# Causal mask of an attention block moved from TensorE to GpSimd, with one copy moved to VectorE and the first batch reordered

## The reference

```python
xn = _layernorm(x, axis=-1)
x = x + _L0_attn_ref(xn, ...) + _L0_ffn_ref(xn, ...)

# attention: 16 heads of 8 channels
qkv = x @ w_in.T + b_in
scores = einsum('bhqd,bhkd->bhqk', q * scale, k) + causal_bias    # -inf above the diagonal
out = einsum('bhqk,bhkd->bhqd', softmax(scores), v) @ w_out.T + b_out

# feed-forward: softmax router, top 2 of 8 experts of width 176, and a shared expert of width 352
g = silu(x @ w_gate) * (x @ w_up)
y = sum over experts of combine * (g @ w_down), and + shared expert
```

## Time and profile before

| | |
|---|---|
| median of 3 runs | 555.38 us (553.04, 557.18, 555.38) |
| the profiled execution, own time | 554.11 us |
| its span | 552.3 us |
| busy share PE, PEld, DVE, ACT, POOL | 93%, 58%, 78%, 60%, 42% |
| one batch (exponential of unit 0 to the next batch's) | 64.8 us: 203.98 to 268.76 |
| of it attend, from the first exponential to the end of the last | 19.2 us: 203.98 to 223.2 |
| granted PE clock, in 40 slices | 0.9 or more of full in all but the third, which has 0.7 |

### The profile page before, as it was taken

The page is one execution under the profiler, slowest core; times in us unless marked ns, Lnnn a source line. Parts: engine busy times, 40 slices in busy tenths (PEclk is TensorE's granted clock), DMA queues, the critical chain, the costliest instruction groups (busy, mean ns, idle before and its releaser), DMA issues.

```text
span 552.3 us, 16880 instructions
## 1 busy us (share of the span) xinstructions
PE 512.5 (93%) x6840; PEld 321.2 (58%) x6840; DVE 430.5 (78%) x845; ACT 330.6 (60%) x454; POOL 229.6 (42%) x201
## 2 busy tenths in 40 slices
PE   1589999999999999999999999999999999999995
PEld 1355654676557664576546664576646765467643
DVE  3989988899859968598757968599686978489713
ACT  6322489445873469544894458834696348844593
POOL 2026810587007840379005870078403790058600
PEclk9979999999999999999999999999999999999999
DMA  9887016900367005750169003770068302590000
GB/s 261 219 242 181 2 67 163 259 5 11 117 188 196 2 11 162 207 132 1 68 170 258 16 11 116 192 193 1 11 188 219 94 1 78 149 270 16 11 21 21
DMA packets 46896, 62.55 MB, mean 113 GB/s; under 512 B 6672, under 2 KB 30448, under 8 KB 46832
## 3 DMA queue, kind: packets, MB, share of 16 engines
q1 hardware_dynamic: 44124, 58.34, 38.6%
q10 hardware_dynamic: 2708, 3.24, 1.8%
HBM read 45.18 MB, written 15.34 MB: 110 GB/s over the span
## 4 chain that ended last, share of the span: by engine, by line
PE 70%; DVE 8%; ACT 7%; issue 5%; DMA 5%; POOL 4%; SPq 1%; ACTq 0%; DVEq 0%
PE banks L577 9%; PE banks L579 8%; PE banks L578 8%; PE banks L613 7%; PE banks L593 7%; PE banks L707 7%; ACT probs L974 5%; PE banks L678 5%; PE banks L594 4%; PE banks L595 4%; DVE neg_max L1273 3%; DMA k_op<-k_dram 2%; POOL hid_lo L1063 2%; PE banks L532 2%; DMA wqk_sb<-in_wqkT 1%
## 5 line engine op out<-in xcount | busy, mean ns | idle before, releaser
L1273 DVE TENSOR_REDUCE neg_max<-banks 128x2 f32<-128x1024 f32 (+7 forms) x240 | 177.9, 790 | 30.1 <-PE banks L604 28.8
L1063 POOL TENSOR_TENSOR hid_lo<-probs,hid_hi 128x512 fp32r<-128x512 f32 x85 | 109.5, 1288 | 214.5 <-ACT hid_hi L911 214.2
L974 ACT ACTIVATE probs<-banks 128x1024 f32<-128x1024 f32 x144 | 139.1, 1026 | 16.4 <-PE banks L691 15.2
L1055 POOL TENSOR_TENSOR probs<-probs,cb 128x512 f32<-128x512 f32 x88 | 113.1, 1285 | 76.1 <-ACT probs L904 75.5
L904 ACT ACTIVATE probs<-banks 128x512 f32<-128x512 f32 (+1 forms) x112 | 66.8, 598 | 124.2 <-PE banks L579 123.1
L1249 DVE TENSOR_TENSOR probs<-probs,banks 128x512 f32<-128x512 f32 (+1 forms) x112 | 75.9, 679 | 33.3 <-POOL probs L1055 24.9
L577 PE MATMUL banks<-x_hi,w_hi 128*128 128x512 f32 (+1 forms) x224 | 95.6, 427 | 4.8 <-DVE probs L1249 4.1
L579 PE MATMUL banks<-x_hi,w_lo 128*128 128x512 f32 (+1 forms) x224 | 89.5, 400 | 0.0
L578 PE MATMUL banks<-x_lo,w_hi 128*128 128x512 f32 (+1 forms) x224 | 88.9, 397 | 0.0
L911 ACT ACTIVATE hid_hi<-probs 128x512 fp32r<-128x512 f32 (+1 forms) x96 | 60.3, 628 | 38.4 <-DVE probs L1249 38.4
L707 PE MATMUL banks<-probs,v_op 64*32 64x512 f32 (+7 forms) x2048 | 78.5, 410 | 0.0
(11 more groups left out here) (138 smaller groups left out, 556.7 us busy)
## 6 DMA issues: line engine op xcount, KB each, us to landing
cb<-c_dram SPq DMA_DIRECT2D x31, 256.0 KB, 4.0
q_op<-q_dram SPq DMA_DIRECT2D x15, 512.0 KB, 6.3
k_op<-k_dram SPq DMA_DIRECT2D x15, 512.0 KB, 7.4
cb<-c_dram SPq DMA_DIRECT2D x16, 224.0 KB, 4.7
q_dram<-q_parts SPq DMA_DIRECT2D x8, 384.0 KB, 2.9
k_dram<-k_parts SPq DMA_DIRECT2D x8, 384.0 KB, 2.6
cb<-c_dram SPq DMA_DIRECT2D x16, 192.0 KB, 3.8
cb<-c_dram SPq DMA_DIRECT2D x15, 160.0 KB, 4.0
```

The lines of the kernel that those rows point to most:

```text
L974: nc.scalar.activation(probs[:, 2 * home_of(n):2 * home_of(n) + 2, :], ring[:, at:at + 2, :], ACT.Exp).then_inc(exp_done, 1)
L1055: nc.gpsimd.tensor_tensor(sg[k % 3][:, :], sg[k % 3][:, :], cb[:, tiles_of(b)[k], :], ALU.mult).then_inc(weighted, 1)
L1063: nc.gpsimd.tensor_tensor(hid_lo[0:n, k % 3, :], hid[k % 3][0:n, :], hid_hi[0:n, k % 3, :].bitcast(F32), ALU.subtract).then_inc(hid_lo_don ...
L1273: return nc.vector.tensor_reduce(out, in_, AX.X, ALU.max, negate=True)
```

## The change

1. **Mask.** `mask_scores_t` and its four matmuls for each unit are gone from `scores_t`. POOL sets the masked elements to zero in the exponentials instead, with `affine_select` in place on `probs`: 64 partitions, four blocks of 64 columns in one instruction. A weighing step has one or two diagonal places and two halves, so 2 or 4 instructions: 2, 4, 4, 4, 2 for w = 0 to 4, that is 32 for a batch. They wait for the exponential of the step's last unit; `weigh_v` now waits for `masked`, not for `exp_done`.
2. **Order.** `WEIGH_BEHIND` is 4 instead of 3, so seven steps go out in the loop and three behind `gate_up(i+1, 0)`. `transpose_y` stands behind unit 5, not 3.
3. **y.** The copy of y out of PSUM is DVE's, between taking q and splitting it; ACT has it no more.
4. **Operands.** The first half of q and k is loaded in two quarters of 256 KB each, and the next batch's first scores wait for the first quarter (`ops_first`) only; unit 4 waits for the second.
5. **First batch.** The three casts of constants and the taking of q are ACT's. DVE scales the query bias behind the router's logits. The tokens of batches 2 to 7 are loaded behind the first `cb` broadcasts.

```diff
-WEIGH_BEHIND = 3
+WEIGH_BEHIND = 4
...
-            tokens_in(1)
-            tokens_in(2)
-            tokens_in(3)
...
-                own = slice(n * PAIRS // 2, (n + 1) * PAIRS // 2)
-                for op, dram in ((q_op, q_dram), (k_op, k_dram)):
-                    sp.dma_start(...).then_inc(ops_loaded[n], 16)
+                parts = [(slice(0, PAIRS // 4), ops_first), (slice(PAIRS // 4, PAIRS // 2), ops_loaded[0])]
+                for own, loaded in (parts if n == 0 else [(slice(PAIRS // 2, PAIRS), ops_loaded[1])]):
+                    for op, dram in ((q_op, q_dram), (k_op, k_dram)):
+                        sp.dma_start(...).then_inc(loaded, 16)
...
             weights_around(2)
+            for n in range(1, 4):
+                tokens_in(n)
...
-                                      q_op[half(a), 2 * g + c, HALF * jk:S], start=(m == 0), stop=False,
-                                      tile_position=(HALF * a, HALF * c), skip_group_check=True)
-                for c in range(2):
-                    for a in range(2):
-                        mm = mask_scores_t(ring[half(c), 2 * ((n + 1) % 2) + a, :], a, c, blocks)
+                                           q_op[half(a), 2 * g + c, HALF * jk:S], start=True, stop=True,
+                                           tile_position=(HALF * a, HALF * c), skip_group_check=True)
                 mm.then_inc(st_ready, 1)
...
-                pe.wait_ge(exp_done, ST_ALL * i + last_unit_of(t, w) + 1)
+                pe.wait_ge(masked, PV_ALL * i + WEIGHINGS * t + w + 1)
...
-                    if n == 3:
+                    if n == 5:
                         transpose_y(i)
...
-                    if n == 1:
-                        take_y(i)
...
             high_routed(1)
+            act.wait_ge(consts_loaded, 16 * 5)
+            nc.scalar.activation(ident_bf[:, :], ident_sb[:, :], ACT.Copy).then_inc(casts_made, 1)
+            nc.scalar.activation(ident_half[:, :], ident_f[:, :], ACT.Copy).then_inc(casts_made, 1)
+            nc.scalar.activation(mask_half[:, :], mask_f[:, :], ACT.Copy).then_inc(casts_made, 1)
             exp_router(0)
+            act.wait_ge(const_made, 1)
+            act.wait_ge(q_ready, 1)
+            nc.scalar.activation(qk_f[:, 0, :], nat[:, 0, :], ACT.Identity, bias=bq_scaled[:, 0:1], scale=QSCALE
+                                 ).then_inc(q_done, 1)
...
+            def mask(units, at):
+                blocks = units.rearrange("p b (k n) -> p b k n", n=HALF)[:, :, at, :]
+                if blocks.shape[1] == 2:
+                    blocks = units.rearrange("p b (h n) -> p (b h) n", h=2)[:, :, 0:HALF]
+                apart(pool, pool_passed)
+                return nc.gpsimd.affine_select(out=blocks, in_=blocks, compare_op=ALU.is_ge, fill=0.0, base=0,
+                                               pattern=[[0, 4], [1, HALF]], channel_multiplier=-1)
+
+            def attend(i):
+                for t in range(GROUPS // 2):
+                    for w in range(WEIGHINGS):
+                        last = last_unit_of(t, w)
+                        first, end = 2 * home_of(TWO_QUADS * t + 2 * w), 2 * home_of(last) + 2
+                        pool.wait_ge(exp_done, ST_ALL * i + last + 1)
+                        for at in ((0, JQ - w) if 0 < w < OWN_UNITS else (0,)):
+                            for c in range(2):
+                                step = mask(probs[half(c), first:end, :], at)
+                        step.then_inc(masked, 1)
...
+            def take_y(i):
+                dve.wait_ge(down_done, NT * i + NT)
+                nc.vector.tensor_copy(yT[:, :], bank_y[:, :]).then_inc(y_taken, 1)
...
                     take_q(i + 1)
+                take_y(i)
+                if front:
                     split_q(i + 1)
```

More of the change, by code:

```diff
@@ L258, in block_kernel @@
         const_made = sem("const_made")
+        casts_made = sem("casts_made")
         wd_loaded = [sem(f"wd_loaded{n}") for n in range(2)]
@@ L312, in block_kernel @@
         exp_done = sem("exp_done")
+        masked = sem("masked")
         pv_done = sem("pv_done")
@@ L452, in operands_in @@
                 apart(sp, sp_passed)
-                own = slice(n * PAIRS // 2, (n + 1) * PAIRS // 2)
-                for op, dram in ((q_op, q_dram), (k_op, k_dram)):
-                    sp.dma_start(op[:, own, :].rearrange("p i n -> p (i n)"),
-                                 dram[:, :, :, own, :].rearrange("t s d i n -> (s d) t (i n)")
-                                 ).then_inc(ops_loaded[n], 16)
+                parts = [(slice(0, PAIRS // 4), ops_first), (slice(PAIRS // 4, PAIRS // 2), ops_loaded[0])]
+                for own, loaded in (parts if n == 0 else [(slice(PAIRS // 2, PAIRS), ops_loaded[1])]):
+                    for op, dram in ((q_op, q_dram), (k_op, k_dram)):
+                        sp.dma_start(op[:, own, :].rearrange("p i n -> p (i n)"),
+                                     dram[:, :, :, own, :].rearrange("t s d i n -> (s d) t (i n)")
+                                     ).then_inc(loaded, 16)
             def store(i):
@@ L673, in scores_t @@
                     pe.wait_ge(exp_done, ST_ALL * i + n - 1)
-                blocks = keys_of(n)
-                for m, (g, jk, at) in enumerate(blocks):
+                for g, jk, at in keys_of(n):
                     for c in range(2):
                         for a in range(2):
-                            pe.matmul(ring[half(c), 2 * ((n + 1) % 2) + a, at:at + S - HALF * jk],
-                                      k_op[half(a), 2 * g + c, HALF * jk:HALF * (jk + 1)],
-                                      q_op[half(a), 2 * g + c, HALF * jk:S], start=(m == 0), stop=False,
-                                      tile_position=(HALF * a, HALF * c), skip_group_check=True)
-                for c in range(2):
-                    for a in range(2):
-                        mm = mask_scores_t(ring[half(c), 2 * ((n + 1) % 2) + a, :], a, c, blocks)
-                mm.then_inc(st_ready, 1)
-            def mask_scores_t(bank, a, c, blocks):
-                second = blocks[-1][2] // HALF
-                diagonal = bank.rearrange("p (k n) -> p k n", n=HALF)[:, 0:second + 1:max(second, 1), :]
-                return pe.matmul(diagonal, mask_half[half(a), :],
-                                 ident_half[half(a), :].unsqueeze(1).to_broadcast([HALF, len(blocks), HALF]),
-                                 start=False, stop=True, tile_position=(HALF * a, HALF * c), skip_group_check=True)
+                            mm = pe.matmul(ring[half(c), 2 * ((n + 1) % 2) + a, at:at + S - HALF * jk],
+                                           k_op[half(a), 2 * g + c, HALF * jk:HALF * (jk + 1)],
+                                           q_op[half(a), 2 * g + c, HALF * jk:S], start=True, stop=True,
+                                           tile_position=(HALF * a, HALF * c), skip_group_check=True)
+                mm.then_inc(st_ready, 1)
             def weigh_v(i, t, w, front):
-                pe.wait_ge(exp_done, ST_ALL * i + last_unit_of(t, w) + 1)
+                pe.wait_ge(masked, PV_ALL * i + WEIGHINGS * t + w + 1)
                 if t == 0 and w == 0:
@@ L954, in experts @@
                         high_hidden(b, k - 1)
-            def take_y(i):
-                act.wait_ge(down_done, NT * i + NT)
-                nc.scalar.activation(yT[:, :], bank_y[:, :], ACT.Copy).then_inc(y_taken, 1)
             def attend(i, front):
@@ L1078, in experts @@
                         place_v(b, i)
+            def mask(units, at):
[15 more added lines that the diff above has]
+                        step.then_inc(masked, 1)
             experts(0, None)
+            attend(0)
             experts(1, 0)
             with pool.Fori(1, NB - 2) as i:
+                attend(i)
                 experts(i + 1, i)
+            attend(NB - 2)
             experts(NB - 1, NB - 2)
+            attend(NB - 1)
         @block.vector
@@ L1503, in _ @@
             router_logits(0, vl_first)
+            dve.wait_ge(qk_weights, 16 * 2)
+            nc.vector.tensor_scalar(bq_scaled[:, :], bqk[:, 0:1], QSCALE, None, ALU.mult).then_inc(const_made, 1)
             dve.wait_ge(bv_loaded, 16 * 2)
```

15 lines of the change are left out of this document (4 added, 11 removed).

## The result

The change takes 561.92 us (median of 4 runs, 561.15 to 562.58), the kernel before 555.01 us (4 runs, 553.04 to 557.18). The ratio is 1.0115, 95% interval 1.0091 to 1.0140: slower by 1.2%. The profiled execution of the change takes 561.15 us with a span of 559.4 us, against 554.11 and 552.3 us before: 7.1 us more.

A forecast was written before the change was run, and what follows sets the result against it. PE binds experts; in attend PE and ACT alternate, neither alone the bound. Seven batches x (1.0 - 0.4) = +4.2, start -1.3, end +0.4: +3.3 us on 554.1, 557.4; forecast 558.5, range 546 to 577.

The forecast's parts named there:

- The end of the stage: End of attend: last exponential at 222.8, gate and up, three weighings of 2.4 us, second natural scores at 226.8.
- That is 0.4 us sooner: End of attend: second natural scores at 226.8 against 227.19 before, a gain of 0.4 us a batch.
- the quarters' "0.85 us": Before the next batch's scores: quarter loads remove PE's 0.85 us pause for the k operand.
- Masks on POOL: Attend: 32 selects of 0.38 us, 12.2 us a batch; four take 1.5 us against 2.2, so weighings don't wait.
- the threshold: POOL in attend: 16 masks in a t's 8.7 us leave 0.54 us each; above that, masks decide.
- POOL beside DVE: Attend: DVE waits beside selects, comb comes 3.8 us later, PE stands there up to 1.3 us; 1.0 charged.
- rival 1: Mask stream in attend: masks and DVE exclude each other, 0.68 us a mask, +13.3 us, 568.7; chance 0.33 with longer tail.
- weighings that wait for POOL: Attend: listed sign that the forecast is wrong, alongside selects of 0.55 us or more.
- y off ACT: Attend: ACT gains 0.5 us without the copy of y, but three waits stay; the stage gains 0.4 us.
- Masks off PE: Attend: removing the mask matmuls frees 1.0 us of PE's queue a batch.
- First batch: Start: casts and taking of q leave DVE, comb comes sooner; 1.3 us gained, bounds 0 and 2.8.
- Last batch: End: three weighings and two masks' rows behind the last exponential, waits for masks; loses 0.4 us.

The follow-up runs named there:

- e2: The change with no causal mask applied at all, weighings waiting only for the exponential: 558.16 us, ratio to the kernel before 1.0040 to 1.0089.
- f4: The kernel before with only the first batch's new order, operands loaded in halves: 553.14 us, ratio 0.9960 to 0.9998.
- e6: The kernel before with the first batch's new order and the quarter loads: 552.86 us, ratio 0.9964 to 0.9992.
- e3: The change with its selects on parts of probs no weighing reads, only a batch's last weighing waiting for them: 559.82 us.
- e7: The change with masks as one 0/1 tensor_tensor product over 128 partitions instead of two selects: 571.25 us, ratio 1.0280 to 1.0323.
- e5: The change with mask matmuls back on PE, no selects, and WEIGH_BEHIND 3: 557.33 us, ratio to the kernel before 1.0042 to 1.0106.
- f2: The change with the copy of y back on ACT and transpose_y back behind unit 3: 561.26 us, ratio 1.0096 to 1.0151.
- f3: The change with no mask applied and WEIGH_BEHIND 3: 553.88 us, ratio to the kernel before 0.9964 to 1.0008.
- e1: The change with WEIGH_BEHIND back at 3, selects kept: 583.06 us, ratio to the kernel before 1.0467 to 1.0555.

## Why the prediction was right, and where its steps were not

The forecast was 558.5 us in a range of 546 to 577, the result 561.9, and slower was its likeliest sign. Against the profiled execution the sum said +3.3 us and +7.1 came. By part: the middle batches +6.6 (forecast +4.2), the start -1.2 (-1.3), the end +1.8 (+0.4). The base of one term was wrong, the last batch was priced too low, and one mechanism was another than forecast.

*The end of the stage.* The forecast put the second natural scores at 226.8, +22.8 after the first exponential, without masks that come late. The kernel in which that is so, e2, has +23.04, with the last exponential at +18.95 (forecast 18.8) and three weighings of 2.44 us (forecast 2.4). That step was sound. What failed is the sentence "That is 0.4 us sooner": it compares with 227.19, from the one stage that I had read, which held the k_op wait of 0.85 us. Against the typical +22.40 the forecast's +22.8 is 0.4 us later, and e2's +23.04 is 0.6 later. Read over seven stages, the quarters' "0.85 us" is 2.0 us in the whole kernel and not 6, and f4 and e6 differ by less than their spread. Nor was the wait gone for good: in the change's fifth stage PE waited 0.34 us for k_op, which cost nothing, as gate and up waited for the last exponential anyway.

*Masks on POOL.* "I take 0.38 us" against 0.41 us (407 at least, median 413 ns): the size was nearly right. But I used a duration for a pitch. And I took it for an idle DVE. In the last batch, where DVE is idle, eight selects take 3.63 us, one every 0.45:

```profile
543.38 3.63 POOL L1078 TENSOR_SCALAR_AFFINE_SELECT probs<-probs 64x256 f32<-64x256 f32 x8 [0.97 <-ACT probs L960]
```

In the middle stages it is 0.53 to 0.54 us on average, just the 0.54 that I had named as the threshold, and up to 0.77 us beside DVE instructions that read two operands in SBUF. "2.2 us, against 4 x 0.38 = 1.5 us: no wait for it" is the step that failed: the 2.2 us of slack were right (219.18 to 221.41), but the four masks of step (1, 1) take 2.58 us. PE waits 0.20 and 0.41 us in a stage, and the second wait reaches the last exponential. Worth 0.67 us a batch (e3 to the change).

*POOL beside DVE.* I charged 1.0 us a batch for PE standing at comb. PE never stood there. comb starts at 217.19 - 204.75 = +12.4 after the first exponential, before at 215.02 - 203.98 = +11.0: 1.4 us later, not 3.8. Without masks (e2) it starts at +11.4, so 0.4 is the copy of y with the new order and 1.0 the selects. PE turns it at 218.81, without a wait. DVE's instructions grew, some little and some by half: those of its form L1239 from 425 to 627 ns,

```profile
L1182 DVE TENSOR_TENSOR q_parts<-qk_rest,q_parts 128x512 bf16<-128x512 f32 x8 | 6.1, 759 | 0.3
...
L1239 DVE TENSOR_TENSOR rt_pair<-rt 128x256 f32<-128x256 f32 x8 | 5.0, 627 | 0.3
```

and the q_parts of L1182 from 693. I had read the earlier trace rows as DVE waiting out whole POOL instructions of 1.25 us; those were two-input ones. By these runs the price is 0.1 to 0.2 us of DVE a piece beside selects and a stop of PE at comb beside two-input products (e7). The Trainium skill, GPSIMD Engine Reference, section 8, has the two contend without a size; the trace agrees in kind (759 ns against 693 for the q_parts). The 1.0 us that I charged lies near the 0.67 us that the masks cost, but through another mechanism; that is luck. The late masks of rival 1, at a pitch of 0.54 and not 0.68, were the mechanism: "weighings that wait for POOL", which I had listed as a sign of being wrong, came. So what came is a mild form of rival 1 within the forecast's range.

*y off ACT.* "ACT gains 0.5 us" is not seen in any run: the move costs 0.4 us (e5) or about 0.1 (f2). *Masks off PE*, 1.0 us of queue, is worth 0.45 to 0.52 us.

*First batch:* forecast -1.3, measured -1.23 in the trace and -1.2 in f4's median. q's split starts at 21.22, before 22.73: 1.5 us, forecast 1.4. The start of the split bears the step out: in all thirteen traces with the new start it lies between 20.9 and 21.5. That the first exponential agrees to the digit is luck. Those thirteen traces have it anywhere from 73.2 to 75.7 us, 74.1 in the middle, and the kernel before has one trace. The first natural scores start only 0.36 us sooner (35.94 against 36.30), since they wait 2.39 us for k_op; where the rest of it is passed on I didn't follow.

*Last batch:* forecast +0.4, measured +1.8, of which 1.4 us are the masks (from its first exponential to the end 29.96 us in the change, 28.51 in e2, 28.18 before). The last weighings wait 0.87 us for their masks and end 549.04 + 1.60 - 529.48 = 21.2 us after that batch's first exponential; before they ended 541.13 + 2.44 - 524.15 = 19.4 us after it. PE's timeline of the change, then of before:

```profile
549.04 1.60 PE L697 MATMUL banks<-probs,v_op 64*32 64x320 f32 x48 [0.87 <-POOL probs L1078]
```

```profile
541.13 2.44 PE L707 MATMUL banks<-probs,v_op 64*32 64x384 f32 x80
```

The typical batch, from the runs: 22.40 before, +0.4 for y and the transposition (e5), -0.45 for the masks off PE (f3), +0.7 for the later order with its third weighing (e2), +0.67 for the late masks (the change) = 23.7.

## What to carry to other kernels

Take the base of a step from all stages that look alike, not from one: one stage with a stall of its own turned a loss of 0.4 us into a gain of 0.4. When work moves to another engine, price the chain from the producer's end to the consumer's start, step by step, with what the neighbour engine runs at that moment: the average pitch of 0.54 us promised four masks in 2.2 us, as much as the slack, and the four that counted took 2.58. And an order that is changed to hide a new latency has a price of its own, here 0.7 us a batch: as much as what was left of the latency, and more than the work that was taken off PE was worth.

## What the runs showed of the hardware

- A select of 64x256 takes 0.41 us, one every 0.45 us with DVE idle, and one every 0.53 to 0.54 us on average in the middle stages. Beside DVE instructions with two operands in SBUF (L1168, L1360) one takes 0.76 to 0.77 us, beside DVE's maxima of scores in PSUM (L1293, from 223.56) 0.41. POOL is slowed by DVE too, which I had excluded for POOL from the earlier trace rows.
- A weighing that waits for a select starts 0.05 to 0.06 us after the select's end (221.76 to 221.82; the fifteen such waits of the change agree).
- A two-input product of 128x256 takes 718 ns at least and 848 in the mean (e7), dearer than the 0.64 us that half of a 128x512 of 1285 ns would give.
- PE's granted clock halves behind some of the long waits, in e7 as in e1. In e7's fourth stage PE waited 1.83 us for comb until 291.27; busy time by stretch afterwards:

```profile
291.00:292.00 1.00, 0.73 (x17) 0.41 (x25) 0.69 (x3) 0.05 (x1) 0.17 (x1) 1.00 0.53 166
292.00:293.00 1.00, 1.00 (x20) 0.16 (x10) 1.00 (x5) 0.97 (x1) 0.00 (x0) 0.92 1.02 293
293.00:294.00 1.00, 1.00 (x24) 0.53 (x28) 0.97 (x2) 0.38 (x1) 0.85 (x2) 0.50 0.89 180
294.00:295.00 1.00, 1.00 (x16) 0.29 (x19) 1.00 (x2) 1.00 (x2) 1.00 (x1) 0.50 0.83 292
```

```profile
293.85 1.96 PE L699 MATMUL banks<-probs,v_op 64*32 64x448 f32 x32
```

At the lower level, 1.2 GHz, a weighing takes 1.96 us instead of 1.10. In the third stage the same wait of 1.83 us (until 224.97) was followed by a clock of 1.00 and a weighing of 1.09 us. So long waits in attend have a second price, paid in some stages and not in others: the third stage's second natural scores start at +24.8, the fourth's at +26.1. The change's own waits, 0.91 us for an exponential at 209.69 the longest of its third stage before gate and up (1.05 us), brought none of it: its granted clock in the stage is 1.00.
